# Decoder kernel on one core: four score products in one group, sums of P split from the weighing in the second block's self attention

## What is computed

```python
q = split_heads(x @ Wq + bq)      # 16 heads of 8
k = split_heads(x @ Wk + bk)
v = split_heads(x @ Wv + bv)
q, k = _rope(q), _rope(k)
scores = jnp.einsum('bhqd,bhkd->bhqk', q, k) / np.sqrt(8)
probs = jax.nn.softmax(scores, axis=-1)
attn = jnp.einsum('bhqk,bhkd->bhqd', probs, v)
out = attn.transpose(0, 2, 1, 3).reshape(B, S, 128) @ Wo + bo
x = _layernorm(x + out)
```

## Time and profile before

| | us |
|---|---|
| median of 3 runs | 2158.24 (2151.73 to 2158.86) |
| the profiled execution's own time | 2157.88 |
| its span | 2156.2 |
| TensorE busy in the span | 1941.1 (90%) |
| VectorE, ScalarE, GpSimd busy | 1422.8, 1230.6, 451.4 |
| the stage of the change, first to last work | about 1403 to 1670 |

### The profile page before, as it was taken

The page is one execution under the profiler, slowest core; times in us unless marked ns, Lnnn a source line. Parts: engine busy times, 40 slices in busy tenths (PEclk is TensorE's granted clock), DMA queues, the critical chain, the costliest instruction groups (busy, mean ns, idle before and its releaser), DMA issues.

```text
span 2156.2 us, 47708 instructions
## 1 busy us (share of the span) xinstructions
PE 1941.1 (90%) x16935; PEld 1503.5 (70%) x16935; DVE 1422.8 (66%) x3526; ACT 1230.6 (57%) x4054; POOL 451.4 (21%) x780
## 2 busy tenths in 40 slices
PE   3548999999999999999869999989998777699998
PEld 1227888888888888888657777667775455467776
DVE  4776777777777777777457667468887577444443
ACT  2215777666666666677424444367776788133343
POOL 2101111111111111111122222034444233011110
PEclk8769999999999999999889999989999799589999
DMA  8000000000000000000200000010000000000000
GB/s 216 24 0 2 2 2 2 2 2 2 2 2 2 2 2 2 2 2 2 69 1 1 1 1 1 1 36 2 3 2 2 26 16 2 1 0 11 6 6 20
DMA packets 29439, 25.65 MB, mean 12 GB/s; under 512 B 5260, under 2 KB 25748, under 8 KB 29208
## 3 DMA queue, kind: packets, MB, share of 16 engines
q1 hardware_dynamic: 29208, 22.62, 4.0%
HBM read 20.52 MB, written 2.10 MB: 10 GB/s over the span
## 4 chain that ended last, share of the span: by engine, by line
issue 63%; PE 21%; POOL 8%; POOLq 6%; DVE 1%; DMA 1%; ACT 0%; DVEq 0%; SPq 0%; ACTq 0%
PE bank L1414 3%; PE bank L1423 3%; PE bank L1435 3%; POOL work L946 2%; PE bank L1942 2%; PE bank L1929 2%; PE bank L1931 2%; POOLq L949 1%; PE bank L1406 1%; POOL H L950 1%; POOL work L934 1%; POOL work L1039 1%; PE bank L1909 1%; POOLq L1822 1%; POOLq L1820 1%
## 5 line engine op out<-in xcount | busy, mean ns | idle before, releaser
L814 ACT ACTIVATE work<-bank,work 128x128 f32<-128x128 f32 x1024 | 364.6, 405 | 223.8 <-DVE work L867 223.8
L694 PE MATMUL bank<-work,wbig 128*128 128x128 f32 x2048 | 261.7, 276 | 0.6 <-ACT work L855 0.5
L814 ACT ACTIVATION_READ_ACCUMULATOR work<-bank,work 128x1 f32 x1024 | 250.4, 245 | 0.0
L694 PEld LDWEIGHTS bank<-work,wbig 128*128 128x128 f32 x2048 | 245.5, 193 | 1.2 <-ACT work L855 0.8
L874 DVE TENSOR_TENSOR work<-work 128x512 f32<-128x512 f32 x256 | 177.3, 692 | 24.4 <-issue 6.4
L867 DVE TENSOR_REDUCE work<-bank 128x4 f32<-128x512 f32 x256 | 158.9, 683 | 33.7 <-PE bank L733 33.7
L829 ACT ACTIVATE work<-bank 128x512 f32<-128x512 f32 x256 | 170.4, 666 | 13.2 <-PE bank L707 13.2
L707 PE MATMUL bank<-ident,work 128*128 128x128 f32 x1024 | 156.4, 276 | 3.0 <-DVE work L874 3.0
L1481 ACT ACTIVATE work<-bank,work 128x128 f32<-128x128 f32 x512 | 147.6, 389 | 9.2 <-DVE work L1513 9.2
L1173 ACT ACTIVATE work<-bank,col_b 128x512 f32<-128x512 f32 x128 | 87.2, 687 | 106.7 <-PE bank L1101 106.5
L707 PEld LDWEIGHTS bank<-ident,work 128*128 128x128 f32 x1024 | 119.2, 141 | 40.3 <-issue 18.9
(11 more groups left out here) (284 smaller groups left out, 4051.5 us busy)
## 6 DMA issues: line engine op xcount, KB each, us to landing
wbig<-in_moe_w SPq DMA_DIRECT2D x2, 1536.0 KB, 9.2
work<-in_mask_l SPq DMA_DIRECT2D x8, 256.0 KB, 2.8
out<-X SPq DMA_DIRECT2D x8, 256.0 KB, 2.3
H<-in_moe_w SPq DMA_DIRECT2D x3, 512.0 KB, 5.6
wff<-in_moe_w SPq DMA_DIRECT2D x1, 1024.0 KB
wbig<-in_sa_wq SPq DMA_DIRECT2D x1, 512.0 KB, 3.7
wbig<-in_sa_wk SPq DMA_DIRECT2D x1, 512.0 KB, 4.5
wbig<-in_sa_wv SPq DMA_DIRECT2D x1, 512.0 KB, 5.8
```

The source lines that it names most:

```text
L694: last = nc.tensor.matmul(o[:, j * T:(j + 1) * T], w[:, t * 128:(t + 1) * 128], src, start=True, stop=True)
L814: last = nc.scalar.activation(at_probs[:, g, h, :], bank[g][:, h * T:(h + 1) * T], ACT.Exp, bias=at_nmax[:, g, h:h + 1], accum_out=at_den[ ...
```

## The change

Three things are done, all inside this stage.

- `score` takes all four groups in one call at the start of a turn. It waits for all four groups of exps of the element before. The call for element t + 1 near the turn's end is gone, and `greatest` for all four groups stands together at the start of VectorE's turn.
- `weigh` is cut in two functions: `total` has the 16 products of the sums and all the waits, `weigh` has the 16 products with v and the signal `pv`. Between them stand the transposes of group 0.
- ScalarE takes the exps of group 0 behind the copy of group 3 and the tokens, and the exps of group 3 ahead of the copy of group 1. VectorE takes the copy of group 2 at the end of its turn instead of at the start of the next.

```diff
-            def score(b, pair):
+            def score(b):
                 pe.wait_ge(l1.kblk, b + 1)
-                need(pe, l1.probs, QUAD * (b - 1) + 2 * pair + 2)
-                for i in (2 * pair, 2 * pair + 1):
+                need(pe, l1.probs, QUAD * b)
+                for i in range(QUAD):
...
-            def weigh(b):
+            def total(b):
                 turned1(pe, b, TURNED_ON_DVE)
                 turned1(pe, b, 3)
                 pe.wait_ge(l1.xT_sb, min(b + 4, B - 1) + 1)
                 pe.wait_ge(l1.v_sb, b + 1)
...
+                for s in range(QUAD):
+                    for j in range(QUAD):
+                        nc.tensor.matmul(bank[7][32 * j:32 * j + 32, T:2 * T], l1_ones[:, s, :], l1_probsT[b % 2][:, j, s, :],
+                                         start=(s == 0), stop=(s == QUAD - 1), skip_group_check=True)
+
+            def weigh(b):
+                for s in range(QUAD):
+                    for j in range(QUAD):
+                        last = nc.tensor.matmul(bank[7][32 * j:32 * j + 32, 0:T], l1_v[b % 3][:, s, 32 * j:32 * j + 32],
+                                                l1_probsT[b % 2][:, j, s, :], start=(s == 0), stop=(s == QUAD - 1),
+                                                skip_group_check=True)
                 last.then_inc(l1.pv, 1)
...
             def greatest(b, g):
-                dve.wait_ge(l1.scores, 2 * b + g // 2 + 1)
+                dve.wait_ge(l1.scores, b + 1)
```

More of the change, by code:

```diff
@@ L1456, in attn1_pe @@
                 if now:
-                    score(t, 1)
+                    score(t)
                 if t >= 1:
@@ L1463, in attn1_pe @@
                     project(t + 2)
+                if t >= 1:
+                    total(t - 1)
                 if now:
@@ L1469, in attn1_pe @@
                     turn(t, 1)
-                if 0 <= t + 1 < B:
-                    score(t + 1, 0)
                 output(t)
@@ L1496, in attn1_act @@
                 now = 0 <= t < B
-                if now:
-                    exps(t, 0)
                 if t >= 1:
@@ L1503, in attn1_act @@
                 if now:
+                    exps(t, 0)
+                if now:
                     exps(t, 1)
@@ L1506, in attn1_act @@
                     exps(t, 2)
+                    exps(t, 3)
                     turned(t, 1)
-                    exps(t, 3)
         def attn1_dve(dve):
             def greatest(b, g):
-                dve.wait_ge(l1.scores, 2 * b + g // 2 + 1)
+                dve.wait_ge(l1.scores, b + 1)
                 nc.vector.tensor_reduce(l1_nmax[b % 2][:, g, :], bank[g][:, :].rearrange("p (h t) -> p h t", h=QUAD),
@@ L1585, in attn1_dve @@
                 now = 0 <= t < B
-                if t >= 1:
-                    turned(t - 1)
                 if now:
-                    greatest(t, 2)
-                    greatest(t, 3)
+                    for g in range(QUAD):
+                        greatest(t, g)
                 if 0 <= t + 2 < B:
@@ L1594, in attn1_dve @@
                     heads(t - 1)
[L1595 to L1598, removed]
                     residual(t - 1)
@@ L1601, in attn1_dve @@
                     values(t + 1)
+                if now:
+                    turned(t)
         def attn1_pool(pool):
@@ L1609, in keys @@
                 pool.wait_ge(l1.turned_halves, b + 1)
-                need(pool, l1.scores, 2 * (b - 1))
+                need(pool, l1.scores, b - 1)
                 nc.gpsimd.tensor_tensor(l1_qk[b % 2], l1_half[b % 2][:, :, 0, :], l1_half[b % 2][:, :, 1, :], ALU.add)
```

## The result

The changed kernel takes 2163.77 us (median of 20 runs, 2161.10 to 2169.08) against 2156.12 for the kernel before (20 runs, 2148.54 to 2159.78, among them the three of the table ahead of the prediction) on the same chips. The ratio is 1.0044 with a 95% interval of 1.0033 to 1.0055: about 7.7 to 9.5 us slower. The time lies in the range of the prediction and the sign is the one it leaned to, but the loss is more than twice the 3.5 us of its sum.

What follows compares the result with a forecast made beforehand. TensorE's queue, busy 40.00 of 40 us, was taken to bound the stage. 28 turns x 0.18 = +5.0, start -2.3 and end +0.8 gave +3.5 us, so 2161.5 us, range 2153 to 2169.

Steps and rivals of the forecast that it cites:

- Part 1: Four score products in one group on TensorE: 1.07 us start to start, the second group's 1.05 us gone.
- Part 2: Sums split from the weighing on TensorE: halves of 1.02 us plus joints add 0.30 us a turn, bounds 0.15 and 0.45.
- Part 3: Heads' chain before the output product loses its cover: 1.52 us instead of 1.64, so only 0.12 us saved.
- The new turn: One turn of TensorE's loop in the changed stage, blocks summed: 7.87 us, +0.18 us a turn.
- Start and end: Both ends of the stage: 2.3 us gained once at the start, 0.8 us lost in the last three turns.
- rival 1: TensorE's clock slips in the stage because of new idle time: 10 us lost, 2171 us; chance 0.10.
- Rival 2: Group 0's transposes wait for the first exps, cover only 0.06 us: 4.6 us more, 2166 us; chance 0.12.
- Rival 3: Gap before the output product filled, turn 6.84 us on TensorE, 7.07 by the exps' loop: 2137 us; chance 0.02.

Runs made afterwards that it cites:

- e3: Changed kernel with two waits of the sums swapped, the wait for v ahead of the late one for the token copy: 2157.06 us, ratio 0.9991.
- e4: Changed kernel with group 2's transposes ahead of the output product and VectorE's copy of group 2 ahead of its residual: 2151.33 us, ratio 0.9968.
- e8: Changed kernel with VectorE's reciprocal replaced by a copy of the same sums: a turn of 7.35 us, 2149.49 us (one run).
- e5: Changed kernel with a one-column exp ahead of ScalarE's loop, so the exps' table loads early: 2164.72 us, ratio 1.0040.
- e1: Changed kernel with the split of sums and weighing undone on TensorE, both behind group 0's transposes: 2184.88 us, ratio 1.0128.
- e6: Changed kernel, sums and weighing together ahead of both transposes, group 2's exps ahead of group 0's copy, plus edits of e3 and e5: 2140.02 us, ratio 0.9933.
- e7: e6 with group 2's transposes ahead of the output product and VectorE's copy of group 2 ahead of its residual: 2144.68 us, ratio 0.9939.
- e9: Changed kernel with only sums and weighing together and ahead of group 0's transposes: a turn of 8.17 us, 2166.01 us (one run).

## Why the prediction was right, and where not

**Part 1** held: four products in one group take 1.14 us, as in the sister stage.

**Part 2** held: sums and weighing are 1.01 each for 1.02, group 0's transposes 0.59 for 0.59, and with the wait moved (e3) the projections 1.01 for 0.98. A joint is never seen by itself, only as such a difference.

**Part 3**, the term with the sign, held to a hundredth: from group 1's transposes to the output product 1.51 us for 1.52, idle 0.86 in each turn as in the last turn of the earlier trace rows. e4 and e8 show that in the changed kernel this chain sets the pace: shorten it by 0.66, and the turn falls by 0.67; fill it with transposes from elsewhere, and the turn falls by 0.44.

**The new turn** was wrong by 0.15 us, 7.87 for 8.02. The step that failed is "The projections thus become 0.89 + 0.09 = 0.98". It priced the joint between the wide and the narrow form, and not that the sums, moved up by the length of group 0's transposes, now arrive just as ScalarE's token copy ends (2.52 behind the score group's start), with four waits ahead of them. The prediction did walk through the covers of the group 0 transposes, of the score group and of the maxima, but not of this wait, which the change moves forward by half a microsecond. e3 shows it: swapping two waits gives 7.88. This is 28 x 0.15 = 4.2 of the 7.5 us missed in the stage. The other 3.3 are at its start and end. That the whole kernel came within 2.3 us of the forecast although the stage was off by 7.5 is partly luck: the forecast starts from 2158.24, the median of three runs, where that of 20 runs is 2156.12, and the traced execution, to which the 7.5 belongs, is 4.9 us above the changed kernel's median.

**Start and end.** At the start -1.4 us for -2.3. The gain of the earlier score group was real, but the table load (1.28 us) came into the open; e5 gives it back. The turn from S(1) to S(2) took 8.77 for 7.87, with a stretch at the lower clock in it (the score group of element 1 takes 1.55 us there instead of 1.14): beyond the 0.15 that is 0.7 more. At the end +2.6 for +0.8. In the last turn the sums wait 0.73 us for VectorE's copy of group 2, but so did the weighing in the kernel before. What differs is the clock. The last sums and weighing, first in the kernel before, then in the changed one:

```profile
1663.09 1.95 PE L1435 MATMUL bank<-work 128*32 128x128 f32 x64 [0.73 <-DVE work L1519]
```

```profile
1674.28 1.80 PE L1433 MATMUL bank<-work 128*32 128x128 f32 x32 [0.73 <-DVE work L1523]
1675.78 2.01 PE L1439 MATMUL bank<-work 128*32 128x128 f32 x32
```

From the start of these products to the reciprocal are 2.01 us before and 3.55 in the changed kernel: 1.5 of the 1.8 us missed at the end. It isn't tied to the changed order: in e3 and e5, where the code is the same but for the order of two waits in e3, the last 16 products with v take 1.08 us, and the part behind S(29) takes 36.2 us instead of 37.8. Without it the end would have been +1.1 for +0.8. What lowered the clock in this one trace stays open; the 0.73 us of idle time ahead of it is shorter than the 0.86 of the turns, which lowered nothing.

**The rivals.** The clock did not slip in the turns: 1.00 in every stretch from 1440 to 1640. By the rule of the Trainium skill that the prediction weighed ("TensorE: Matmul & The Clock Gate", section on psum-queue depth-cycling), gaps of this kind could have made it go back and forth; this trace does not show that: 0.86 us of idle time in each turn left the clock at its upper level. At both ends of the stage the lower clock did cost something, outside the place that rival 1 named. Rival 2 (group 0's transposes wait for the first exps) did not occur in the changed kernel: its transposes follow the sums at 1.01. The late start of the sums had widened their cover, but in e3, where it is gone, they follow at 1.01 too. In e1, where the cover was taken away, the wait is there. Rival 3, the filled gap, is what e4 and e6 built in another way than by an earlier reciprocal; the 7.07 that it gave for the exps' loop is 7.30 in e6 and e7.

## What to carry to other kernels

Before work is taken off the busiest engine, ask what was waiting in its shadow: the score pair covered most of a chain of 1.5 us through VectorE (a reciprocal and a product), and without it the engine idled for almost as long as it had worked. Look for a place in the trace where the cover is already missing (here the last turn of the loop); it gives the new wait to a hundredth. When a block is moved earlier in a queue, go through each of its waits for how early it was fulfilled, and put the one that comes last at the end of the row. Once a gap is filled, look for the loop that is next: here it was ScalarE's exps, 0.7 us below the changed kernel's turn.

## What the runs showed of the hardware

**The order of waits in TensorE's queue is worth 0.15 us when one of them is late.** e3 differs from the changed kernel by the order of two waits, 8.02 and 7.88 us a turn. From the end of the token copy to the start of the sums are 0.25 us (14 turns) or 0.35 (10 turns) with a fulfilled wait behind the late one, and 0.14 (24 turns) with the late one last. I had counted a handover at 0.05. Why it is 0.25 in some turns and 0.35 in others stays open.

**Halves cost more than half.** 16 products of 128x32 take 1.01 us to the next block when another form follows, and 0.88 when more of the same follow (e6, 1541.53 to 1542.41).

**The part behind the changed stage comes in several lengths.** Outside the changed stage the profiled runs differ though nothing in the code does: from the sister stage's first transpose to the end it is 479.2 us in the changed kernel and 474.6 in e3. Most of the difference lies in how long the clock stays low between some 160 and 230 us into that part. The same stretch, first of the changed kernel, then of e3, each from 211 us behind the sister stage's first transpose (columns: window, length, busy time of the five engines, granted clock):

```profile
1899.00:1919.00 20.00, 17.30 (x53) 10.36 (x53) 8.37 (x18) 5.65 (x11) 4.33 (x6) 0.73 0.00 0
```

```profile
1892.00:1912.00 20.00, 17.59 (x66) 11.33 (x67) 10.39 (x24) 6.15 (x13) 5.78 (x8) 0.87 0.00 0
```

Over all traces this part takes from 472.8 us (e9) to 481.1 (before). That is more than the effects of e3 or e5, and not far below the 11.2 us over which the 20 runs of the kernel before spread. So effects of this size were read from the turns, which repeat to 0.1 us, and not from the total. What decides how long the clock stays low there stays open.
